# Expert stage's down products nine steps behind instead of six, and norms from maxima and squares instead of Gram products

## What is computed

```python
def _gemma_mlp(x, gate_w, up_w, down_w):
    g = x @ gate_w                  # 128 -> 512
    u = x @ up_w                    # 128 -> 512
    return (gelu(g, approximate=True) * u) @ down_w    # 512 -> 128
rw = softmax(router_logits); w, sel = top_k(rw, 2); w = w / w.sum()
out = sum over experts e of dense_w[:, e] * _gemma_mlp(x, skill_gate[e], skill_up[e], skill_down[e])
out = out + _gemma_mlp(x, shared_gate, shared_up, shared_down)
return x + out
```

## Time and profile before

| what | us |
|---|---|
| median of 3 executions | 213.76 |
| the profiled execution, its own time | 213.64 |
| its span, first to last instruction | 211.9 |
| PE busy | 206.8 |
| ACT busy | 134.3 |
| DVE busy | 124.7 |
| POOL busy | 107.7 |

### The profile page before, as it was taken

The page is one execution under the profiler, slowest core; times in us unless marked ns, Lnnn a source line. Parts: engine busy times, 40 slices in busy tenths (PEclk is TensorE's granted clock), DMA queues, the critical chain, the costliest instruction groups (busy, mean ns, idle before and its releaser), DMA issues.

```text
span 211.9 us, 6739 instructions
## 1 busy us (share of the span) xinstructions
PE 206.8 (98%) x2735; PEld 167.2 (79%) x2736; DVE 124.7 (59%) x223; ACT 134.3 (63%) x217; POOL 107.7 (51%) x109
## 2 busy tenths in 40 slices
PE   7999999999999999999999999999999999999995
PEld 2445555555443467899999999999999999999995
DVE  3387995788999998644434435435344344444452
ACT  6253585889978998556565565565565655655650
POOL 3000444444564667765656556556556565565562
PEclk9999999999999999999999999999999999999999
DMA  6999600000000000000010010010010010010011
GB/s 204 414 437 421 260 2 0 3 0 0 2 3 0 0 0 5 3 3 2 3 51 5 3 50 3 3 50 5 0 54 3 3 50 6 2 53 3 3 50 53
DMA packets 2813, 11.70 MB, mean 55 GB/s; under 512 B 352, under 2 KB 608, under 8 KB 2400
## 3 DMA queue, kind: packets, MB, share of 16 engines
q1 hardware_dynamic: 2640, 11.01, 12.9%
q10 hardware_dynamic: 144, 0.26, 0.5%
HBM read 9.18 MB, written 2.10 MB: 53 GB/s over the span
## 4 chain that ended last, share of the span: by engine, by line
PE 90%; DVE 6%; DMA 2%; issue 1%; POOL 1%; SPq 0%; DVEq 0%; POOLq 0%
PE o_ps L612 7%; PE g_ps L594 7%; PE u_ps L594 7%; PE o_ps L611 7%; PE u_ps L593 7%; PE g_ps L593 7%; PE o_ps L610 7%; PE g_ps L592 7%; PE u_ps L592 7%; PE n_ps L528 3%; PE o_ps L573 3%; PE o_ps L575 2%; PE o_ps L574 2%; PE u_ps L560 2%; PE u_ps L562 2%; PE u_ps L561 2%
## 5 line engine op out<-in xcount | busy, mean ns | idle before, releaser
L258 POOL TENSOR_TENSOR h<-h 128x512 f16<-128x512 f32 x92 | 106.0, 1158 | 99.7 <-ACT h L290 49.4
L412 DVE SCALAR_TENSOR_TENSOR h<-gel,sk_factor,u_ps 128x512 f32<-128x512 f32 x64 | 47.8, 747 | 67.8 <-PE u_ps L594 38.2
L285 ACT ACTIVATE gel<-g_ps,sk_gate 128x512 f32<-128x512 f32 x64 | 44.0, 687 | 49.6 <-PE g_ps L594 49.6
L290 ACT CAST h<-h 128x512 f16<-128x512 f32 x92 | 56.1, 609 | 3.9 <-DVE h L412 3.7
L593 PE MATMUL g_ps<-x,wsk 128*128 128x128 f16 x256 | 46.2, 219 | 0.0
L593 PE MATMUL u_ps<-x,wsk 128*128 128x128 f16 x256 | 46.2, 219 | 0.0
L594 PE MATMUL g_ps<-x,wsk 128*128 128x128 f16 x256 | 46.2, 219 | 0.0
L594 PE MATMUL u_ps<-x,wsk 128*128 128x128 f16 x256 | 46.2, 219 | 0.0
L592 PE MATMUL u_ps<-x,wsk 128*128 128x128 f16 x256 | 46.2, 219 | 0.0
L592 PE MATMUL g_ps<-x,wsk 128*128 128x128 f16 x256 | 46.2, 219 | 0.0
L611 PE MATMUL o_ps<-h,wsk 128*128 128x128 f16 x256 | 45.9, 219 | 0.0
(11 more groups left out here) (97 smaller groups left out, 303.7 us busy)
## 6 DMA issues: line engine op xcount, KB each, us to landing
wsk<-skills SPq DMA_DIRECT2D x3, 2048.0 KB, 16.0
outT<-xT SPq DMA_DIRECT2D x7, 256.0 KB, 3.8
xT<-xT SPq DMA_DIRECT2D x2, 768.0 KB, 6.5
wsh<-shared SPq DMA_DIRECT2D x3, 256.0 KB, 3.6
xT<-xT ACTq DMA_DIRECT2D x1, 256.0 KB, 3.2
xT<-xT SPq DMA_DIRECT2D x1, 256.0 KB, 4.9
outT<-xT SPq DMA_DIRECT2D x1, 192.0 KB, 1.9
outT<-xT SPq DMA_DIRECT2D x1, 64.0 KB, 1.6
```

What stands on the lines that cost most here:

```text
L258: nc.gpsimd.tensor_tensor(hidden_lo(t), hidden_full(t), hidden_hi(t), ALU.subtract).then_inc(lo_ok, 1)
L285: nc.scalar.activation(gel[:, t % NG, :], g_ps[t % 2][:, :], ACT.Gelu_apprx_tanh, scale=scale).then_inc(gelu_ok, 1)
L290: nc.scalar.copy(hidden_hi(t), hidden_full(t)).then_inc(hi_ok, 1)
L412: nc.vector.scalar_tensor_tensor(out=h32[:, t % N32, :], in0=gel[:, t % NG, :], scalar=factor, in1=u_ps[t % 2][:, :], op0=ALU.mult, op1=AL ...
```

## The change

Nine steps instead of six lie between an expert's gate and down products; `lag` rises at steps 33, 35 and 37 as well, and the hidden tile has ten buffers instead of seven. The norms of `x` and of the shared weights no longer come from Gram products: DVE takes each partition's largest absolute value (11 reductions over 128 x 512 float32), squares them, and PE sums them over the partitions with two matmuls of 1, 3 or 4 columns. The experts' down norm comes from ACT: four squares with a sum per partition, each over 1024 of the 4096 columns of float32. 76 of the 140 Gram matmuls go. K_GATE and K_UP keep theirs. The masks of the norm groups, the `x` splits and the splits of the experts' down weights stand in other steps, routing's spread moves from the start to step 4, the skill tables from step 22 to 24.

```diff
-    LAG = 6
+    LAG = 9
-        GRAM_AT = {2: X_NEXT, 4: X_REST}
-        K_STEPS = [5, 9, 13]
-        MASK_AT = {1: FIRST, 2: X_NEXT, 4: X_REST, 8: K_GATE, 12: K_UP, 16: K_DOWN}
-        SPREAD_AT = {3: X_NEXT, 5: X_REST, 9: K_GATE, 13: K_UP, 17: K_DOWN}
+        TOP_AT = {1: (1,), 3: (2, 3), 5: (4, 5), 6: (6, 7)}
+        TOP_OF = {FIRST: 4, X_NEXT: 7, X_REST: 11}
+        K_STEPS = [5, 9]
+        MASK_AT = {3: X_NEXT, 6: X_REST, 8: K_GATE, 12: K_UP, 22: K_DOWN}
+        SPREAD_AT = {4: X_NEXT, 7: X_REST, 9: K_GATE, 13: K_UP, 23: K_DOWN}
+        SQUARES_AT = {11: 0, 13: 1, 17: 2, 21: 3}
-        X_AT = {4: 1, 6: 7, 8: 2, 10: 3, 13: 4, 15: 5, 17: 6}
+        X_AT = {5: 1, 8: 7, 9: 2, 10: 3, 15: 4, 19: 5, 23: 6}
-        PIECES = {12 + 2 * n: n for n in range(3 * E // EG)}
+        PIECES = {t: n for n, t in enumerate((12, 14, 16, 18, 20, 22, 24, 26, 29, 32, 35, 38))}
         def lag(t):
-            return 3 if t < 12 else 4 if t < 18 else 5 if t < 24 else LAG
+            return 3 if t < 12 else 4 if t < 18 else 5 if t < 24 else 6 if t < 33 else 7 if t < 35 else 8 if t < 37 else LAG
...
+            def squares(n):
+                if n == 0:
+                    act.wait_ge(sk_in[DOWN], 16)
+                unused = wsk[:, (4 * E + 2 * n) * I:(4 * E + 2 * n + 2) * I]
+                part = wsk32[:, (2 * E + 2 * n) * I:(2 * E + 2 * n + 2) * I]
+                nc.scalar.activation(unused.bitcast(BF16), part, ACT.Square, accum_out=sq_sum[:, n:n + 1]).then_inc(sq_ok, 1)
...
-                if t == 4:
+                if t == 3:
                     shared_high(DOWN)
                 if t > C:
                     cast(t - 1)
+                if t in SQUARES_AT:
+                    squares(SQUARES_AT[t])
                 if t in X_AT:
                     x_high(X_AT[t])
...
+            def tops(col, src):
+                nc.vector.tensor_reduce(top[:, col:col + 1], src, AX.X, ALU.max, apply_absolute_value=True).then_inc(top_ok, 1)
...
             def mask(n):
                 a, b = COLS[n]
+                if n < K_GATE:
+                    dve.wait_ge(top_ok, TOP_OF[n])
+                    nc.vector.tensor_tensor(top2[:, a:b], top[:, a:b], top[:, a:b], ALU.mult).then_inc(diag_ok, 1)
+                elif n < K_DOWN:
...
+                else:
+                    dve.wait_ge(sq_ok, E // 2)
+                    nc.vector.tensor_scalar(sq_floor[:, :], sq_sum[:, :], NORM_FLOOR, None, ALU.add).then_inc(diag_ok, 1)
...
             def scales(n):
+                norm = n_ps[1][:, 0:b - a]
+                if n >= K_GATE:
+                    norm = n_all[:, a:b]
+                    nc.vector.tensor_reduce(norm, n_ps[1][:, 0:E // 2 if n == K_DOWN else P], AX.X, ALU.max).then_inc(n_red, 1)
...
             routing_weights()
+            for q in (GATE, UP, DOWN):
+                top_shared(q)
+            top_x(0)
+            mask(FIRST)
             for t in range(STEPS):
                 hidden(t)
...
+                if t == 0:
+                    scales(FIRST)
+                    shared_tables(0, 1, 1)
+                if t in TOP_AT:
+                    for j in TOP_AT[t]:
+                        top_x(j)
                 if t in MASK_AT:
                     mask(MASK_AT[t])
...
+                if t == C:
+                    routing_spread()
-                if t == 22:
+                if t == 24:
                     skill_tables()
-                if t == 8:
+                if t == 10:
                     add_group(0)
...
             def spread_norms(n):
                 a, b = COLS[n]
                 pe.wait_ge(diag_ok, n + 1)
+                if n < K_GATE:
+                    sums = n_ps[1][:, 0:b - a]
+                    nc.tensor.matmul(sums, ones[:, :], floor[:, 0:b - a], start=True, stop=False)
+                    nc.tensor.matmul(sums, ones[:, :], top2[:, a:b], start=False, stop=True).then_inc(norm_ok, 1)
...
             gate_up_first(0, GATE)
-            gram(n_ps[0][:, P:2 * P], wsh32[:, 0:I], True)
             pe.wait_ge(sh_in[UP], 16)
             gate_up_first(0, UP)
-            gram(n_ps[0][:, 2 * P:3 * P], wsh32[:, I:2 * I], False)
             gate_up_first(1, GATE)
+            gate_up_first(1, UP)
+            pe.wait_ge(consts, 3)
+            spread_norms(FIRST)
+            gate_up_first(2, GATE)
+            gate_up_first(2, UP)
             pe.wait_ge(sh_in[DOWN], 16)
-            gram(n_ps[0][:, 0:P], wsh32[:, 2 * I:3 * I], False)
-            pe.wait_ge(x_in[1], 16)
-            gram(n_ps[0][:, 3 * P:4 * P], xT32[:, 0:GN], False).then_inc(gram_ok, 1)
-            gate_up_first(1, UP)
-            gate_up_first(2, GATE)
-            pe.wait_ge(consts, 2)
-            spread_norms(FIRST)
-            gate_up_first(2, UP)
             down_first(0)
```

More of the change, by code:

```diff
@@ L25 @@
 NORM_FLOOR = float(2.0 ** -40)
+ROW_FLOOR = NORM_FLOOR / P
 def build(nc, xT, cond, skills, shared, outT):
@@ L70, in build @@
         ident = sb("ident", [P, P], F32)
-        diag = sb("diag", [P, 4, P], BF16)
+        floor = sb("floor", [P, 4], BF16)
+        diag = sb("diag", [P, P], BF16)
+        sq_sum = sb("sq_sum", [P, E // 2], F32)
+        sq_floor = sb("sq_floor", [P, E // 2], BF16)
         DC, GC, UC, XC, KC = 0, 1, 2, 3, 3 + G
@@ L76, in build @@
         n_all = sb("n_all", [P, NS], F32)
+        top = sb("top", [P, NS], F32)
+        top2 = sb("top2", [P, NS], BF16)
         e_bits = sb("e_bits", [P, NS], U32)
@@ L133, in build @@
         r_words = sem("r_words")
+        top_ok = sem("top_ok")
         gram_ok = sem("gram_ok")
+        sq_ok = sem("sq_ok")
         diag_ok = sem("diag_ok")
@@ L243, in _ @@
             nc.gpsimd.memset(ones[:, :], 1.0).then_inc(consts, 1)
+            nc.gpsimd.memset(floor[:, :], ROW_FLOOR).then_inc(consts, 1)
             nc.gpsimd.memset(ident[:, :], 0.0).then_inc(zeroed, 1)
@@ L327, in _, with top_shared, top_x @@
         def _(dve):
+            def tops(col, src):
+                nc.vector.tensor_reduce(top[:, col:col + 1], src, AX.X, ALU.max, apply_absolute_value=True).then_inc(top_ok, 1)
+            def top_shared(q):
+                dve.wait_ge(sh_in[q], 16)
+                tops((GC, UC, DC)[q], wsh32[:, q * I:(q + 1) * I])
+            def top_x(j):
+                dve.wait_ge(x_in[0 if j == G - 1 else 1 if j == 0 else 2 if j < XA else 3], 16)
+                tops(XC + j, xT32[:, j * GN:(j + 1) * GN])
             def mask(n):
                 a, b = COLS[n]
[L330 to L334, removed]
+                if n < K_GATE:
+                    dve.wait_ge(top_ok, TOP_OF[n])
+                    nc.vector.tensor_tensor(top2[:, a:b], top[:, a:b], top[:, a:b], ALU.mult).then_inc(diag_ok, 1)
+                elif n < K_DOWN:
+                    dve.wait_ge(gram_ok, n - K_GATE + 1)
+                    nc.vector.scalar_tensor_tensor(out=diag[:, :], in0=n_ps[0][:, 0:P], scalar=NORM_FLOOR, in1=ident[:, :],
+                                                   op0=ALU.add, op1=ALU.mult).then_inc(diag_ok, 1)
+                else:
+                    dve.wait_ge(sq_ok, E // 2)
+                    nc.vector.tensor_scalar(sq_floor[:, :], sq_sum[:, :], NORM_FLOOR, None, ALU.add).then_inc(diag_ok, 1)
             def scales(n):
@@ L338, in scales @@
                 dve.wait_ge(norm_ok, n + 1)
[L339 to L342, removed]
+                norm = n_ps[1][:, 0:b - a]
+                if n >= K_GATE:
+                    norm = n_all[:, a:b]
+                    nc.vector.tensor_reduce(norm, n_ps[1][:, 0:E // 2 if n == K_DOWN else P], AX.X, ALU.max).then_inc(n_red, 1)
+                    dve.wait_ge(n_red, n - K_GATE + 1)
+                nc.vector.tensor_scalar(e_bits[:, a:b], norm.bitcast(U32), 1, EXP_MASK,
                                         ALU.logical_shift_right, ALU.bitwise_and).then_inc(s_step, 1)
@@ L454, in routing_weights, with routing_spread @@
                                                in1=w_live[:, :], op0=ALU.mult, op1=ALU.add).then_inc(r_step, 1)
+            def routing_spread():
                 dve.wait_ge(r_step, 10)
@@ L481, in _ @@
                     skill_low(PIECES[t - 1])
+                if t == 0:
[4 more added lines that the diff above has]
+                        top_x(j)
                 if t in MASK_AT:
                     mask(MASK_AT[t])
-                if t == 1:
-                    scales(FIRST)
-                    shared_tables(0, 1, 1)
                 if t == 2:
@@ L534, in spread_norms @@
                 pe.wait_ge(diag_ok, n + 1)
-                nc.tensor.matmul(n_ps[1][:, 0:(b - a) * P], ones[:, :], diag[:, 0:b - a, :].rearrange("p k i -> p (k i)"),
-                                 start=True, stop=True).then_inc(norm_ok, 1)
+                if n < K_GATE:
+                    sums = n_ps[1][:, 0:b - a]
+                    nc.tensor.matmul(sums, ones[:, :], floor[:, 0:b - a], start=True, stop=False)
```

(18 more changed lines are left out.)

2 lines of the change are left out of this document (1 added, 1 removed).

## The result

| | before, same session | after |
|---|---|---|
| median | 213.82 us (213.72 to 214.72, 4 executions) | 216.33 us (215.97 to 217.32, 4 executions) |
| ratio | | 1.0115, 95% interval 1.0071 to 1.016 |
| the profiled execution, its span | 213.64, 211.9 | 216.57, 214.7 |
| mean granted clock | 1.000 | 0.992 |

The change makes the kernel slower, by 2.5 us; the forecast was 213.0. In a second session the same kernel took 214.8 us (213.93 to 216.60, 7 executions, ratio 1.0048, interval 1.0013 to 1.0083). The two sessions differ for one reason that the records show: an execution of this kernel has a mean granted clock of 1.000 or of 0.992. The first session had four of four at 0.992, the second two of seven (215.89 and 216.60, against 213.93 to 214.99 for the other five, median 214.63).

What follows compares the result with a forecast made beforehand. PE was taken to bound the kernel, busy in 98% of the span. Gain 6.26 less 2.85 (step 7), 1.5 (step 23), 1.1 (one mask behind POOL) and 0.1 is 0.7: 213.0 us, range 210.6 to 214.4.

Steps and rivals of the forecast that it cites:

- At no cost: Longer lag, later row-group stores, maxima on DVE in steps 1 and 3 and one more POOL memset: priced at nothing.
- LAG 9: Nine-step lag in the expert steps and tail: said to cost nothing, at most 3 x 0.8 us if its cover failed.
- Loss A: Step 7: PE waits at the X_REST spread for DVE's queued mask, 2.85 us, 1.1 more if POOL is first.
- What leaves PE: 76 Gram matmuls (4.37 us), smaller spreads (0.41) and old waits (1.48) leave PE: gain 6.26 us together.
- The start: Up to step 4: no wait at the first spread, x group 0 landing near 7.5, gate of step 4 near 15.6.
- B: The gate start of step 4; DVE's queue from there ends the X_REST mask at B + 9.14 before holds.
- Loss B: Step 23: PE waits at the K_DOWN spread behind ACT's squares and DVE's queue, 1.5 us (1.1 to 1.6).
- C + 26.4: End of the K_DOWN mask with DVE's own queue, counted from C, the gate start of step 11.
- ACT's lateness alone: ACT's full queue would stop gate 25 until C + 27.3 or so; already covered by other waits, not counted twice.
- that rival (223): Squares on ACT need another activation table than gelu; loads put 10.3 us on ACT: about 223, chance 0.03.
- neither is held: Rival: neither the X_REST nor the K_DOWN mask is held by POOL; gain 1.8 us, 211.9, chance 0.27.
- The skill tables: Tables now at step 24, with hidden(25) behind them, reach up of step 27 about when PE does: 0.1 us lost.

Runs made afterwards that it cites:

- e8: Changed kernel with x maxima 4 and 5 and first add_group earlier, routing's spread earlier, K_DOWN spread later, lag six with earlier pieces: 210.11 us, ratio 0.9813.
- a0: The changed kernel run again unedited in a second session: 214.8 us, five of seven executions at full clock.
- e4: Kernel before the change with only the nine-step lag and what it needs, pieces left in place: 214.87 us, ratio 1.003.
- e9: e8 with the nine-step lag and the pieces of the change: 211.94 us, ratio 0.9904.
- e1: Changed kernel with twelve matmuls of zeros before the X_REST spread in step 7: 214.28 us, ratio 1.0004.
- e3: Changed kernel with the first add_group in step 9 instead of 10: 213.4 us, ratio 0.9974.
- e10: e8 with K_DOWN's norm from 32 Gram matmuls and no squares on ACT: 211.03 us, ratio 0.9845.
- e5: Changed kernel with K_DOWN's mask in step 24, spread in 25 and skill tables in 26: 216.95 us, ratio 1.0109.
- e6: Changed kernel with lag six and the last four pieces back at steps 28 to 34: 215.31 us, ratio 1.0059.
- e7: Changed kernel with K_DOWN's norm from 32 Gram matmuls again, no squares, maxima kept: 215.88 us, ratio 1.0106.
- e2: Changed kernel with the maxima of x groups 4 and 5 in step 3 instead of 5: 213.09 us, ratio 0.9946.
- e11: e8 with the skill tables in step 28 instead of 24: 210.45 us, ratio 0.9816.

## Why the prediction was wrong

Two steps of it failed. "At no cost" put `add_group(0)` and LAG 9 at nothing: 1.33 us, and 0.8 with the pieces. And Loss A's "That is 1.9 us of waiting" stopped where PE goes on: in the recorded executions 1.64 us at half the clock came behind the wait. The rest of the 216.57 is a slow first product, 0.9 us.

**What leaves PE: right.** Steps 12 to 23 take 63.46 - 39.66 = 23.80 us, less the wait of 1.17 that is 22.63, where they took 24.42 before: 1.79 less, for 32 Gram matmuls that were priced at 1.84. `e8` shows what the gain is worth when most waits are gone.

**The start: right in `a0`, late in other executions.** In `a0` and the recorded profile the first spread did not wait, and the gate of step 4 stood at 15.56 and at 16.48. In the ten profiles of edits of the changed kernel (`e4` keeps the old start) it lies between 15.48 and 16.65, by two things. One is the length of the first product: it is nearly all that sets `e9` (16.40) apart from `e8` (15.48). The other is the landing of `x` group 0, put at 7.5: its maximum began at 7.08 in `a0`, at 7.64 in `e1`, at 8.62 in `e3` and at 8.59 in `e10`, and in the last three the first spread waited 0.34, 0.54 and 0.83 us for it. The prediction has this among its signs of being wrong, and no price for it.

**Loss A, step 7: the mechanism right, the price incomplete.** DVE's queue came out as added up: `B` + 9.14 + 0.83 + 0.1 is 26.55 for `B` = 16.48, and the mask was done at 26.43. The rows of DVE and POOL:

```profile
20.04 1.14 DVE L411 TENSOR_SCALAR sh_factor<-s_bits 128x3 f32<-128x3 f32 x1
21.21 0.68 DVE L500 TENSOR_SCALAR spread<-ident,route 32x32 f32<-32x32 f32 x4
...
24.96 1.26 DVE L352 TENSOR_REDUCE top<-xT 128x1 f32<-128x512 f32 x2
26.26 0.17 DVE L366 TENSOR_TENSOR top<-top 128x4 bf16<-128x4 f32 x1
```

```profile
19.96 1.19 POOL L271 TENSOR_TENSOR h<-h 128x512 f16<-128x512 f32 x1 [17.41 <-ACT h L303]
25.18 2.27 POOL L271 TENSOR_TENSOR h<-h 128x512 f16<-128x512 f32 x2 [4.04 <-DVE x L393]
```

POOL's low part of step 4 did hold a table operation, `sh_factor`, for 0.9 us, and routing's spread came late behind it; PE waited 0.44 and 2.16, 2.6 together against the 2.85 of the forecast. The mask at 26.26 took 0.17: not held. It came 0.04 us before POOL's second part (26.30), on the side that the prediction gave 0.27. The two maxima at 24.96, beside POOL, took 1.26 us, as the pair at 22.46 did with POOL idle. By the Trainium skill, SBUF — State Buffer, section "Who interferes with whom", a `tensor_reduce` does not contend with GpSimd; the trace agrees. What the step left out is what an engine with a 2 us hole in its work loses afterwards. The failed words are "That is 1.9 us of waiting": they end where PE goes on. Six of the runs keep this hole (the recorded one, `a0`, `e3`, `e5` to `e7`): 22 of their 36 executions have the lower mean clock, and in the profiles that show it the fall stands just behind the hole and costs 1.64 us. With the hole filled (`e1`) or 0.8 us long (`e2`, `e8` to `e11`) none of 41 has it.

**Loss B, step 23: the size about right, its worth not.** 1.17 us for a forecast of 1.5. There was no idle on ACT from 41.09 to 68, and a square costs what was put down.

```profile
59.91 1.08 ACT L315 ACTIVATE wsk<-wsk 128x1024 bf16<-128x1024 f32 x1
60.87 0.21 ACT L315 ACTIVATION_READ_ACCUMULATOR wsk<-wsk 128x1 f32 x1
60.97 0.70 ACT L298 ACTIVATE gel<-g_ps,sh_gate 128x512 f32<-128x512 f32 x1
```

1.06 from square to next operation, less than the 1.25. What came last before the mask was DVE's own queue, as the prediction's C + 26.4 has it: the last sum is read by 61.08 and gelu(22) is done at 61.67, but `hidden(22)` stands behind a held `skill_low` and an `add_group`.

```profile
60.23 1.68 DVE L399 SCALAR_TENSOR_TENSOR wsk<-wsk,s_bits 128x1024 f16<-128x1024 f32 x1
...
62.50 0.73 DVE L453 SCALAR_TENSOR_TENSOR h<-gel,sh_factor,u_ps 128x512 f32<-128x512 f32 x1
63.15 0.15 DVE L373 TENSOR_SCALAR sq_floor<-sq_sum 128x4 bf16<-128x4 f32 x1
```

But this wait is not on the chain that ended last. That chain leaves PE at the gate of step 12, goes over ACT's full queue from 40.51 to 63.83 (the 11% of the page), the squares in it, changes to DVE behind gelu(23) and comes back to PE only at up of step 27 (start us, us, what):

```profile
60.04 1.05 ACT wsk L315 x2
...
63.22 0.59 ACT gel L298
63.83 0.75 DVE h L453
...
70.28 0.39 PE u_ps L618
```

So the 1.17 and the 0.34 of the skill tables are one loss, and removing the first only makes the second longer, as `e8` shows. The prediction named this path in "ACT's lateness alone", but ended it at the gate of step 25. This mask took 0.15 and was not held either, again by little: POOL's second part began at 63.17. No table load stands beside a square, so that rival (223) falls. By the two masks the case was "neither is held", 211.9: 2.1 us under `a0` at full clock.

**At no cost: wrong, and the largest failure.** Two edits in this list, or missing from it, were on the path.
- `add_group(0)` went from step 8 to step 10, and the prediction named no price for it. It frees `o_ps[0]` for the group that PE starts in step 11, and behind `hidden(10)` and an `x_low` it ends too late:

```profile
35.83 0.75 DVE L453 SCALAR_TENSOR_TENSOR h<-gel,sh_factor,u_ps 128x512 f32<-128x512 f32 x1 [0.52 <-PE u_ps L620]
36.50 0.74 DVE L393 SCALAR_TENSOR_TENSOR x<-xT,s_bits,x 128x512 f16<-128x512 f32 x1
37.16 0.68 DVE L464 SCALAR_TENSOR_TENSOR xT<-o_ps,xT 128x512 f32<-128x512 f32 x1
```

  1.33 us; `e3` moves it one step and the wait is gone.
- "LAG 9": DVE was not counted. The sum covered ACT, POOL and the buffers. But the first expert down now comes just before the last piece is split (0.28), and with an odd lag a row's `add_row` asks for DVE behind `hidden(95)` in the tail (0.49). `e4` measures 0.6 to 0.8 us and `e6` 1.0 for lag and pieces.

**The skill tables: 0.1 forecast, 0.34 measured.** One of them met POOL and took 1.14. `e11` moved them away in `e8` and won nothing.

**The sum again.** Neither mask held: 211.84 for the profiled execution by the prediction. With 1.33 + 0.78 + 0.24 for the missed places and 0.25 and 0.33 less for A and B this is 213.6; `a0` took 213.99. The half clock and the slow start, 2.5 us, make it the 216.57 of the recorded one. That `a0`'s profiled execution lies inside the stated range of 210.6 to 214.4 is no success of the mechanism: the missed places added 2.35 us, and the sum stayed in the range because neither mask was held, by 0.04 and 0.02 us. That is luck.

## What to carry over

Work taken from the busiest engine is won only if the engine that takes it over delivers before the busiest one's turn: add up that engine's queue to the consumer, as with Losses A and B, and then move its items until they fit, which made 1.2% slower into 1.9% faster here. A wait that can be seen on PE is not always its own price: if another engine's queue is full over the same steps, as ACT's was here, the wait only moves to the next place where PE needs it. Go through every line of the diff that moves an instruction and ask who reads or reuses what it frees; the one that is not asked about costs as much as the ones that are. A wait on PE of 2 us may cost nearly as much again at a lower clock behind it, and in only some executions, so look at the granted clock of each execution before two medians are compared.

## What the runs showed of the hardware

- The fall of the clock is not a property of the program alone: the same waits were followed by 0.50 for 3.4 us in one execution and by 1.00 in another. The kernels with the hole had it in 4 of 4, 2 of 7, 4 of 10, 3 of 4, 7 of 7 and 2 of 4 executions. What decides it is not shown. In the three profiles where it fell (the recorded one, `e5`, `e6`) the first product had taken 1.72 to 1.83 us, in the three where the hole stood at full clock (`a0`, `e3`, `e7`) 0.93 to 1.33; whether the two hang together is open.
- The first float32 product takes up to 0.9 us longer in some executions, with a granted clock of 1.00 in the records and no wait named. `e4`, an edit of the kernel before, has a part of it (1.22 from its start to the next matmul, instead of 0.94); its cause is open.
- Operations of DVE on a few columns beside POOL: `sh_factor` (128x3) at 20.04 took 1.14 us and was done when POOL was. Two reductions over 128x512 from SBUF at 24.96 passed beside POOL unheld.
